# Attention and feed-forward kernel on one core: bias columns and mask loaded later, weight pieces earlier, and a new order of the work on all engines

## The reference, cut to what matters

```python
x = x + xattn(layernorm(x), ctx, ctx, mask, wq, bq, wk, bk, wv, bv, wo, bo)   # 16 heads of 32
x = x + bitffn(layernorm(x), w1, b1, w2, b2)

def xattn(q, k, v, ...):
    Q, K, V = q @ wq + bq, k @ wk + bk, v @ wv + bv
    scores = where(mask == 0, 1e-9, Q K^T / sqrt(32))
    return (softmax(scores) @ V) @ wo + bo

def bitlinear(x, w, b):                  # w1: 2048 x 512, w2: 512 x 2048
    xq = act_quant(rmsnorm(x))           # 8 bits, one scale per row
    wq = weight_quant(w)                 # -1, 0, 1 times mean |w| over the whole matrix
    return xq @ wq.T + b
bitffn(x) = bitlinear(gelu(bitlinear(x, w1, b1)), w2, b2)
```

## Time and profile before, and how to read it

| | |
|---|---|
| median of 3 runs | 657.68 us |
| profiled execution, its time / its span | 658.44 / 656.6 us |
| TensorE busy | 633.1 us, 96% of the span |
| VectorE / ScalarE / GpSimd busy | 576.7 (88%) / 530.0 (81%) / 517.0 (79%) us |
| mean granted TensorE clock | 0.997 of full speed |
| read from and written to device memory | 35.12 MB, 8.39 MB |

### The profile page before, as it was taken

One profiled execution on the slowest core, in us unless ns is written; L12 is line 12 of the kernel. 1 busy time (PEld: TensorE's weight loads), 2 busy tenths in 40 slices (PEclk: granted clock), 3 DMA queues, 4 the chain that ended last, 5 costly groups with the idle time before them and its releaser, 6 DMA issues.

```text
span 656.6 us, 14114 instructions
## 1 busy us (share of the span) xinstructions
PE 633.1 (96%) x4904; PEld 424.6 (65%) x4904; DVE 576.7 (88%) x1062; ACT 530.0 (81%) x1450; POOL 517.0 (79%) x653
## 2 busy tenths in 40 slices
PE   8888999999999999999999999999999999899996
PEld 7656886665566776666667766666766766556532
DVE  6678889998999989999799989999898889999995
ACT  2379678887898878888988878888888889988782
POOL 3198985979866999669966989669967878889966
PEclk9999999999999999999999999999999999999999
DMA  8982420423124433072244533053333212524236
GB/s 286 404 277 119 127 42 9 105 43 102 33 58 121 120 73 73 10 182 82 41 73 100 143 72 73 9 153 80 72 73 73 69 28 73 115 58 117 57 61 176
DMA packets 109285, 65.38 MB, mean 100 GB/s; under 512 B 90855, under 2 KB 90855, under 8 KB 108575
## 3 DMA queue, kind: packets, MB, share of 16 engines
q1 hardware_dynamic: 108159, 64.49, 37.7%
q10 hardware_dynamic: 1056, 0.00, 0.1%
HBM read 35.12 MB, written 8.39 MB: 66 GB/s over the span
## 4 chain that ended last, share of the span: by engine, by line
PE 54%; POOL 18%; DVE 13%; issue 5%; DMA 4%; ACT 4%; SPq 2%; POOLq 0%; DVEq 0%
PE ps_a L561 19%; PE ps_y L698 10%; PE ps_z L675 9%; PE ps_t L634 6%; POOL prob L2246 4%; PE ps_s L624 3%; POOL hid L2257 3%; PE ps_a L646 3%; DVE hs L1620 2%; POOL q_h L2262 2%; DMA raw_wk_h<-in_L_ffn_w_dram 2%; DVE hid L1612 2%; ACT prob L1133 2%; POOL xn L2202 2%; PE ps_a L595 2%
## 5 line engine op out<-in xcount | busy, mean ns | idle before, releaser
L1133 ACT ACTIVATE prob<-ps_s,nmax 128x120 f32<-128x120 f32 x512 | 178.8, 375 | 31.4 <-DVE nmax L1566 25.0
L2246 POOL TENSOR_TENSOR prob<-prob,pinv 128x480 f32<-128x480 f32 x128 | 128.8, 1012 | 51.1 <-DVE pinv L1571 50.5
L675 PE MATMUL ps_z<-w1T,q_xT 128*128 128x512 fp8e4 x476 | 122.7, 380 | 4.4 <-DVE hid L1612 3.5
L1133 ACT ACTIVATION_READ_ACCUMULATOR prob<-ps_s,nmax 128x1 f32 x512 | 112.7, 220 | 0.0
L698 PE MATMUL ps_y<-w2T,q_hT 128*128 128x512 fp8e4 x448 | 104.0, 379 | 0.3 <-DMA q_hT<-q_h 0.3
L1612 DVE SCALAR_TENSOR_TENSOR hid<-ps_z,y_deq,b_row 128x512 f32<-128x512 f32 x119 | 88.0, 740 | 12.9 <-PE ps_z L675 10.8
L1109 ACT COPY probT<-ps_t 120x512 f32<-120x512 f32 x128 | 76.7, 599 | 26.8 <-PE ps_t L634 23.4
L1563 DVE COPY_PREDICATED_SCALAR ps_s<-hidden_key,masked_c 128x480 f32 x128 | 90.5, 707 | 3.4 <-PE ps_s L624 3.4
L1566 DVE TENSOR_REDUCE nmax<-ps_s 128x4 f32<-128x480 f32 x128 | 84.1, 657 | 4.4
L634 PE MATMUL ps_t<-ident,prob 128*120 128x128 f32 x512 | 78.2, 275 | 2.4 <-POOL prob L2246 2.3
L634 PEld LDWEIGHTS ps_t<-ident,prob 128*120 128x120 f32 x512 | 59.8, 137 | 24.0 <-issue 6.2
(11 more groups left out here) (207 smaller groups left out, 1379.7 us busy)
## 6 DMA issues: line engine op xcount, KB each, us to landing
x<-in_x_dram SPq DMA_DIRECT2D x32, 256.0 KB, 3.0
out_dram<-x SPq DMA_DIRECT2D x32, 256.0 KB, 2.7
xn<-in_x_dram SPq DMA_DIRECT2D x7, 1024.0 KB, 6.5
hid<-in_L_ffn_w_dram SPq DMA_DIRECT2D x4, 1024.0 KB, 8.7
ctx_k<-in_ctx_dram SPq DMA_DIRECT2D x8, 240.0 KB, 3.9
ctx_k<-in_mask_Bx1xSxS_ik_dram SPq DMA_DIRECT2D x7, 240.0 KB, 3.5
xn<-in_x_dram SPq DMA_DIRECT2D x4, 256.0 KB, 4.8
x<-in_L_xattn_wq_dram SPq DMA_DIRECT2D x1, 1024.0 KB, 8.4
```

What stands on the lines that cost most here:

```text
L675: last = nc.tensor.matmul(bank[:], q_xT[:, k % 3, i], w1T[:, i, c * CH:(c + 1) * CH], start=(i == 0), stop=(i == KD - 1))
L1133: last = nc.scalar.activation(prob[:, n % 3, g * S2:(g + 1) * S2], ps_s[n % HG][:, g * S2:(g + 1) * S2], ACT.Exp, bias=nmax[:, n % 4, g:g ...
L2246: gp.tensor_tensor(pr, pr, pinv[:, n % 4].unsqueeze(2).to_broadcast([P, HG, S2]), ALU.mult).then_inc(s["prob_ready"], 1)
```

## The change

No instruction is added, removed or resized, but for one wait on ScalarE. All five lists are put into a new order. In the opening: ScalarE issues the two bias columns only when the third x tile has landed. SP loads piece 1 first (before 0, 3 and 2), and the mask of batch 0 and the row bo, which stood ahead of the last of these pieces, come later: the mask behind wo, bo behind piece 7. On TensorE turn_keys(0) comes ahead of first_q and the fourth turn_xn(0,3) behind the projection of the keys; on ScalarE evac_q(0,0) ahead of both sums; on VectorE split_wq behind the first xT_low, scale_bq behind the sum of piece 1, hide(0) behind the statistics of batch 1, split_wo ahead of invert_sums(0).

```diff
 @ SyncE
             for t in range(T):
                 sp.dma_start(xn[:, t], xt_v[0, t]).then_inc(s[f"first{t}_in"], 16)
...
+            load_first_ctx()
+            load_wq()
+            load_wk()
+            load_piece(1)
             load_piece(0)
             load_piece(3)
-            load_piece(1)
-            load_bias(bo, bo_row)
             load_piece(2)
             load_x(1)
             load_wo()
+            load_first_mask()
             load_wv()
             load_piece(4)
+            load_next_ctx()
             load_bv()
-            load_next_ctx()
-            load_residual(0)
+            load_piece(5)
             load_piece(6)
-            load_piece(5)
             load_residual(1)
             load_piece(7)
+            load_bias(bo, bo_row)
             load_bias(b1, b1_row)
             load_bias(b2, b2_row)
+            load_residual(0)
             load_x(2)
             load_residual(2)
+            load_mask(1)
+            load_residual(3)
             load_residual(5)
-            load_residual(3)
-            load_mask(1)
...
             for a in range(2, 6):
+                store(4 * a - 6)
                 turn_x(4 * a - 3)
-                store(4 * a - 6)
...
 @ TensorE
             turn_xn(0, 2)
+            project_ctx(0, "k")
             turn_xn(0, 3)
-            project_ctx(0, "k")
+            turn_keys(0)
             first_q(0)
             first_q(1)
             first_q(2)
             project_q(0, 1)
             project_q(0, 2)
             total_weights(0)
-            turn_keys(0)
             project_q(0, 3)
+            scores(0)
             turn_piece(0, (0, 1))
-            scores(0)
             turn_piece(0, (2, 3))
...
             turn_probs(24)
+            ffn_up(3, 1)
             attend(5)
-            ffn_up(3, 1)
-            turn_ctx(3)
             scores(7)
+            ffn_down(1, 0)
+            ffn_down(1, 1)
             ffn_up(3, 2)
             turn_probs(25)
             project_q(2, 2)
+            turn_ctx(3)
...
                 project_out(4 * a - 2)
+                turn_xn(a + 1, 1)
                 ffn_up(4 * a - 3, 0)
                 turn_probs(16 * a - 2)
-                turn_xn(a + 1, 1)
...
 @ ScalarE
+            act.wait_ge(s["first2_in"], 16)
             for v, dst in ((bq, bq_col), (bk, bk_col)):
                 act.dma_start(dst[:], v.rearrange("(g p) -> p g", p=P), allow_slow_non_contiguous=True
                               ).then_inc(s["bias_col_in"], 16)
...
             evac_turn(("x", 0, 2))
+            evac_keys(0)
             evac_turn(("x", 0, 3))
+            evac_q(0, 0)
             sum_abs(0)
-            evac_keys(0)
             sum_abs(2)
-            evac_q(0, 0)
...
 @ VectorE
-            scale_bq()
+            xT_low(0, 0)
             split_wq()
-            hide(0, mask0_in)
-            xT_low(0, 0)
             xT_low(0, 1)
             xT_low(0, 2)
             xT_low(0, 3)
             sum_abs(1)
+            add_bk(0)
+            scale_bq()
             sum_abs(3)
             weight_scales(0)
...
+            hide(0, mask0_in)
+            softmax_max(0)
             evac_piece(0, 1)
-            softmax_max(0)
+            split_wo()
+            invert_sums(0)
             evac_piece(0, 3)
             softmax_max(1)
-            invert_sums(0)
-            split_wo()
...
             softmax_max(11)
+            hide(1, mask_in)
+            evac_piece(5, 1)
...
             evac_piece(6, 1)
-            ln1_stats(2, 3)
-            hide(1, mask_in)
             evac_piece(6, 3)
...
 @ GpSimd
             for a in range(2, 6):
+                y_factor(4 * a - 3)
                 round_x(4 * a - 3)
                 normalize(16 * a - 2)
+                add_bo(4 * a - 1)
                 h_factor(4 * a - 5)
-                add_bo(4 * a - 1)
-                y_factor(4 * a - 3)
...
+                ln1_factors(a + 2, 0, 4, 3 * a + 9)
+                normalize(16 * a + 10)
+                round_h(4 * a - 2)
+                add_b2(4 * a)
                 add_bo(4 * a + 1)
-                round_h(4 * a - 2)
-                ln1_factors(a + 2, 0, 4, 3 * a + 9)
                 round_x(4 * a)
...
```

More of the change, by code:

```diff
@@ L832, in _ @@
             scores(5)
+            turn_xn(2, 2)
             turn_probs(17)
             project_out(3)
+            turn_probs(18)
             turn_xn(2, 3)
-            turn_probs(18)
             ffn_up(1, 2)
@@ L956, in _ @@
             project_ctx(7, "k")
+            ffn_up(21, 1)
             ffn_down(19, 0)
+            ffn_down(19, 1)
             turn_probs(96)
-            ffn_up(21, 1)
             attend(23)
-            ffn_down(19, 1)
+            turn_xn(7, 2)
             ffn_up(21, 2)
+            scores(25)
             turn_probs(97)
-            turn_xn(7, 2)
-            scores(25)
             ffn_up(21, 3)
-            turn_probs(98)
             project_out(23)
@@ L1967, in _ @@
-                ln2_stats(4 * a)
                 ln1_stats(a + 2, 1)
                 ln1_stats(a + 2, 2)
+                residual(4 * a)
+                invert_sums(16 * a + 8)
+                invert_sums(16 * a + 9)
+                softmax_max(16 * a + 11)
+                add_bk(a + 1)
+                evac_up(4 * a - 1, 0)
                 ln1_stats(a + 2, 3)
+                invert_sums(16 * a + 10)
+                hide(a + 1, mask_in)
                 h_scale(4 * a - 2)
+                ln2_stats(4 * a)
@@ L2339, in _ @@
             normalize(9)
-            round_x(0)
-            y_factor(0)
             round_piece(4)
@@ L2344, in _ @@
             normalize(10)
-            ln1_apply((0, 1))
+            round_x(0)
             normalize(11)
             normalize(12)
+            ln1_apply((0, 1))
+            y_factor(0)
+            normalize(13)
             ln1_apply((2, 3))
-            normalize(13)
+            round_x(1)
             add_b2(0)
             normalize(14)
-            round_x(1)
             y_factor(1)
+            add_bo(2)
             normalize(15)
-            add_bo(2)
+            add_b2(1)
             normalize(16)
@@ L2358, in _ @@
             add_bo(3)
-            add_b2(1)
+            add_bo(4)
+            round_x(2)
+            add_bo(5)
+            normalize(18)
             y_factor(2)
-            normalize(18)
-            round_x(2)
             normalize(19)
+            normalize(20)
             round_h(0)
-            normalize(20)
             h_factor(0)
+            add_b2(2)
+            y_factor(3)
             normalize(21)
+            round_x(3)
             normalize(22)
-            add_b2(2)
-            round_x(3)
-            add_bo(4)
-            add_bo(5)
+            add_b2(3)
             round_h(1)
-            y_factor(3)
             ln1_factors(3, 0, 4, 12)
```

772 lines of the change are left out of this document (382 added, 390 removed).

## The result

The changed kernel's profiled execution took 650.6 us (span 648.8), where the one before took 658.44 (656.6). Its ratio to the kernel before is 0.989 [0.9866, 0.9914]. Measured a second time, it took 650.93 us (median of four) against 658.12 (of nine): 0.9893 [0.9879, 0.9906], **7.2 us faster**. The first four executions hold one of 713.32 us, and the kernel before has one of 1281.38 in a later measurement, that were disturbed and are in no ratio. The forecast was 655.8, its range 652.0 to 661.0: the kernel came out faster than the range allowed, by 1.1 us. The nearest rival is (a), 652.4.

What follows compares the result with a forecast made beforehand. TensorE was taken as full from 60 to 100 and 200 to 540, with GpSimd's chain gating the start. Terms -1.3 (start), -1.6 (turn_ctx(3)) and +1.0 (hide(1)) made -1.9: 655.8 us from median 657.68, range 652.0 to 661.0.

Steps and rivals of the forecast that it cites:

- (a): Start, hide(1) and ending: wk lands 0.9 us or more earlier, mask in time, half the 540-604 gaps filled; 652.4, chance 0.30.
- Mask and bo row behind the pieces: Opening, SP queue: piece 2 lands 1.26 us earlier, but TensorE becomes late, total_weights(0) at about 28.25; -0.5.
- turn_keys(0) ahead of first_q: Opening, TensorE: first_q starts at 19.05, 1.78 us later, which limits the start's gain to 0.5.
- Bias columns: Opening, behind three x tiles: x up to 1.76 us earlier, wk taken as 0 (1.76 earlier to 0.5 later).
- split_wo, -0.8: Opening, VectorE: with split_wo ahead of invert_sums(0), normalize(0)'s wait of 0.82 us goes; -0.8.
- The clock, costed at nothing: Opening, TensorE: no 1.2 GHz drop without the 2.26 us gap; project_q(0,3) ends some 3 us earlier, covered by GpSimd, 0.
- turn_ctx(3), -1.6: Middle, TensorE: moved later, it gives evac_down(1) some 4 us more and its wait goes; -1.6, bounds -1.6 and 0.
- hide(1), +1.0: Middle, VectorE: ahead of evac_piece(5,1) it waits for its mask and delays piece 5; +1.0, bounds 0 to +2.3.
- The loop, 0: Four loop rounds: y_factor ahead of round_x on GpSimd, offset by work moved away; 0, bounds -0.8 to +6.1.
- The ending, 0 (-2 and +2): From 540 to 604, grouped with other loop moves and last waits: swaps of neighbours, 0, bounds -2 and +2.
- Rival (b): Loop: ffn_up(4a-3,0) waits for q_x each round, 1.53 us each, 6.1 in all; 661.9, chance 0.17.

Runs made afterwards that it cites:

- mask and bo row late alone: Kernel before, with the first mask behind wo, the bo row behind piece 7 and hide(0) behind ln1_stats(1,3): 656.64 us, 0.9976.
- loop alone: The change's orders only in the four rounds of the loop, the old orders elsewhere: 658.02 us, 0.9999.
- opening and middle: The change's opening and middle orders together, with the old loop and ending: 652.65 us, 0.9923.
- split_wo back: The changed kernel with split_wo on VectorE behind softmax_max(1) again: 650.82 us, 0.9888.

## Why the prediction was wrong in size

The sign of its sum was right and its place, the start, in part; it had -1.9 where -7.2 came. Three steps of it failed. The two terms of the middle, -1.6 and +1.0, make -0.6 where -3.0 was there. The ending was put at 0 and gave -1.2. And in the opening the step that cut the transfers' 1.26 to 0.5 did not hold. Step by step:

- **Mask and bo row behind the pieces**: right in the transfer. 1.26 us was the price, and putting them back cost 1.4; piece 2's sum started at 24.73 instead of 26.67, where about 25.4 was said (24.71 to 25.50 over the eight traces with the new opening and these two late). What failed is the step behind it, "TensorE itself becomes the late one and total_weights(0) runs at about 28.25", which cut this to **-0.5**: it ran at 26.80, and at 26.77 to 27.55 over the eight. The chain from the keys' projection to first_q was right (4.88 us by the forecast's steps, 4.92 from 13.43 to 18.35). But the projection began 0.74 earlier than in the profile of before (13.43, not 14.17), as wk landed 9.7 us after its issue, not 10.5. That is in part the columns' new place (0.35 by the medians) and in part chance; it was not tried by itself. And the products take less: the forecast set 3.43 + 5.76 = 9.19 as TensorE's own work, and from 18.35 to 26.80 they take 8.45. first_q's three groups take 2.88 now (18.35 to 21.23), so a part of the 3.43 was not TensorE's own; in before VectorE's xT_low, which the second group reads, ended at 18.68, 0.05 ahead of that group. 28.25 less 0.70 for the start (19.05 to 18.35) and 0.74 for the products is the measured 26.8.
- **turn_keys(0) ahead of first_q**: costs nothing; without it TensorE waits 0.84 for the sum over piece 2 instead.
- **Bias columns**: 0 taken, and no difference found in the time. wk lands some 0.35 earlier with the columns late, by the medians of all traces; most of the bandwidth lost ahead of 5 us came back as lost behind it.
- **split_wo, -0.8**: the wrong cause. Most of the wait of 0.82 was the leftover of a clock that had fallen; 0.17 is what it is otherwise, it is gone with the mask and bo row late alone, and split_wo's place changes nothing. The row was read rightly and taken for the order's doing. Against that one profile there was something to win here, but it was the clock's, the next term. That the sharing's 1.95 would just meet the rounding was right.
- **The clock, costed at nothing**: it cost 0.64 where it fell, in the profile of before and three more. "GpSimd's two passes over the first piece cover it" is wrong by that much: scores(0) came later, its sums too, and normalize(0) waited.
- **turn_ctx(3), -1.6**: wrong in mechanism. Moved alone, it gave 0; its wait belonged to h_factor(1) on GpSimd, and with that one put forward to GpSimd's whole row. The -3.0 of the middle came from all five lists, and which moves in them make it is open. I had named evac_down(1) as the late one without asking what it waited for: "issue" was the answer of the view, and I did not look up h_deq.
- **hide(1), +1.0**: not there. I reckoned its issue "two issues earlier", at 77.7. It came at 73.98, as SP waited for an x slot that the turning of piece 5 frees, and that came 3.3 us earlier. With the old place the stall is there and costs more than I took (2.8 by the median, against 1.0 with 2.3 as its bound).
- **The loop, 0**: right for the loop alone (0.9999). Behind the new middle the lead grows by 0.86 from tile 5 to 27 with the new loop and by 0.36 with the old one (opening and middle), so some half of a microsecond comes in there. Rival (b) is dead: from 200 to 540 TensorE idles 0.5 us.
- **The ending, 0 (-2 and +2)**: -1.2 by the lead, -1.1 to -1.7 by the medians. I had said that swaps of neighbours are worth nothing; here they turned 2.95 us of waiting for evac_up into 0.41, of which new waits for transposes took back the most.

Rival (a) had the time nearly, 652.4, and its sign, total_weights(0) before 27.5, was there (26.80). Of its three conditions hide(1) finding its mask held as put. wk landed 0.8 earlier in the pair of profiles, where 0.9 was asked, and by the medians 0.35. Half of the ending's gaps came in, behind 555 rather than in 540 to 604 alone. That the sum comes out near is in part luck: it has 1.6 for the middle, which gave 3.0.

By the lead the two profiles differ by 7.8 us: 2.85 at tile 0, of which 0.64 is the clock of that one execution of before, 2.85 from there to tile 5, 0.86 to tile 27 and 1.2 behind it. The medians give 7.2. Of this, shown by runs are 1.3 to 1.4 by the mask and bo row (from both sides), 3.0 in the middle as a block by the profiles (2.1 by the medians where it is alone) and 1.1 to 1.3 in the ending as a block. What is left, 1.5 to 1.8 us, has no run of its own. It holds the half microsecond of the loop, the rarer drop of the clock, and an earlier start that is within what executions of one order differ by (0.8 for total_weights(0)).

## What to carry to other kernels

A wait that the profile shows at one instruction may belong to the row of work of another engine: moving the waiting instruction, or even the one that it waits for, hands the wait to the next in the row. Follow it to the engine that is late all along before pricing it. Of orders that were made together for several engines, single steps or one engine's list gave nothing here, or a loss, while two transfers moved at the start paid by themselves. To find where such a change pays, cut all lists at points that both orders pass. Before pricing a stall of half a microsecond, look whether other executions of the same order have it at all.

## What the runs showed of the hardware that was not expected

The same order of work had its clock lowered in four profiled executions, behind gaps of 1.70 to 2.30 us, and kept in five, behind gaps of 1.25 to 2.29. By the mean clock it was lowered in 51 of 93 executions of the kernel before, at 0.7 us. With the 1056 small packets of the columns issued behind the third x tile instead of at the start, the x tiles landed 1.15 us earlier, wq 0.6 and wk 0.35, by the medians of twenty traces: the gain shrinks from transfer to transfer. And the price of VectorE and GpSimd at work side by side did not go by the size of GpSimd's instruction in the two cases here: beside VectorE's split_wo (128x2048) the rounding (128x2048) took 3.81 instead of 1.90, and with split_wo back normalize (128x480) took 2.91 instead of 0.99, each 1.9 longer. VectorE's split itself took 3.63 in the first, where it had begun beside the rounding step ahead, 2.61 in the second, and 2.26 in before, beside normalize alone.
